# The input regions of a deformable convolution, turned once ahead of the loop instead of once in every step

## The reference

```python
x = x + _L0_conv_ref(_gn(x), ...)   # Fourier mixing along each axis plus a 1x1 mixing
x = x + _L1_conv_ref(_gn(x), ...)   # modulated deformable 3x3 convolution

# _L1_conv_ref, cut:
om   = conv3x3(x, w_om) + b_om              # 27 maps: dy, dx and a mask for each of 9 taps
mask = sigmoid(om[:, 18:])
ys, xs = dy + ky + row - 1, dx + kx + column - 1
vals = bilinear_sample(x, ys, xs) * mask    # 4 corners, zero outside the image
out  = einsum('bckhw,ock->bohw', vals, weight) + bias
```

## Time and profile before

| quantity | value |
|---|---|
| median of 3 runs | 2316.26 us (2314.34 to 2319.66) |
| profiled execution | 2315.21 us |
| its span, first to last instruction | 2313.2 us |
| mean granted TensorE clock | 0.968 |
| busy: PE, DVE, ACT, POOL | 1873.3, 1571.6, 1730.5, 1373.4 us |
| bytes moved by DMA | 363.82 MB, 58% of the engines' span |

### The profile page before, as it was taken

The page is one execution under the profiler, slowest core; times in us unless marked ns, Lnnn a source line. Parts: engine busy times, 40 slices in busy tenths (PEclk is TensorE's granted clock), DMA queues, the critical chain, the costliest instruction groups (busy, mean ns, idle before and its releaser), DMA issues. The chain is left out here.

```text
span 2313.2 us, 126528 instructions
## 1 busy us (share of the span) xinstructions
PE 1873.3 (81%) x50241; PEld 1302.3 (56%) x50241; DVE 1571.6 (68%) x2558; ACT 1730.5 (75%) x3238; POOL 1373.4 (59%) x1803
## 2 busy tenths in 40 slices
PE   8566178888888888888888888888888888888885
PEld 3411056666666666666666666666666666666663
DVE  8699166767676766676666666666666667676763
ACT  0003378888888888888888888888888888888884
POOL 0000066676667666766676676677667766766662
PEclk9599589999999999999999999999999999999997
DMA  8036536666666666666566666656665666666653
GB/s 323 1 127 281 224 90 158 157 154 157 159 152 158 156 161 152 156 156 162 151 157 154 153 159 156 160 153 156 156 161 152 157 158 155 157 156 159 153 155 89
DMA packets 196542, 363.82 MB, mean 157 GB/s; under 512 B 39760, under 2 KB 122480, under 8 KB 192368
## 3 DMA queue, kind: packets, MB, share of 16 engines
q1 hardware_dynamic: 196464, 362.74, 58.0%
HBM read 159.38 MB, written 52.22 MB: 91 GB/s over the span
## 5 line engine op out<-in xcount | busy, mean ns | idle before, releaser
L731 DVE COPY big<-pE 128x768 f32<-128x768 f32 x768 | 718.1, 935 | 190.3 <-PE pE L944 168.2
L478 POOL TENSOR_TENSOR halves<-prod,halves 128x300 f16<-128x300 f32 x768 | 604.0, 786 | 322.0 <-ACT halves L559 321.9
L565 ACT ACTIVATE big<-pE 128x768 f32<-128x768 f32 x768 | 632.2, 823 | 105.4 <-PE pE L944 100.0
L965 PE MATMUL pV<-big 128*32 128x144 f32 x16384 | 663.9, 291 | 7.2 <-issue 4.2
L469 POOL TENSOR_TENSOR prod<-big 128x300 f32<-128x300 f32 x768 | 550.2, 716 | 100.8 <-POOL big L493 32.2
L944 PE MATMUL pE<-big,sel_s 32*128 32x64 f16 (+1 forms) x24576 | 409.1, 202 | 241.4 <-DVE big L731 168.8
L944 PEld LDWEIGHTS pE<-big,sel_s 32*128 32x128 f16 x24576 | 325.7, 92 | 451.4 <-issue 311.8
L718 DVE STREAM_TRANSPOSE big<-halves 128x384 f32<-128x384 f32 x768 | 437.6, 570 | 173.3 <-POOL halves L478 171.3
L965 PEld LDWEIGHTS pV<-big 128*32 128x32 f32 x16384 | 436.4, 109 | 55.1 <-issue 10.1
L559 ACT ACTIVATE halves<-prod 128x300 f16<-128x300 f32 x768 | 452.9, 590 | 3.4 <-POOL prod L469 3.3
L493 POOL TENSOR_TENSOR big<-big,msk 128x360 f32<-128x360 f32 x128 | 105.0, 821 | 478.4 <-ACT big L579 478.4
(11 more groups left out here) (72 smaller groups left out, 1123.7 us busy)
## 6 DMA issues: line engine op xcount, KB each, us to landing
v<-big SPq DMA_DIRECT2D x1536, 96.0 KB
win<-xh_scratch SPq DMA_DIRECT2D x128, 544.0 KB, 4.2
big<-xh_scratch SPq DMA_DIRECT2D x384, 136.0 KB, 4.1
xh_scratch<-win SPq DMA_DIRECT2D x32, 544.0 KB, 2.7
big<-in_x SPq DMA_DIRECT2D x16, 1024.0 KB, 16.5
x_scratch<-big SPq DMA_DIRECT2D x16, 1024.0 KB, 3.9
x1r<-x_scratch SPq DMA_DIRECT2D x128, 128.0 KB, 2.1
out<-outs SPq DMA_DIRECT2D x128, 128.0 KB, 1.8
```

What stands on the lines that cost most here:

```text
L478: nc.gpsimd.tensor_tensor(half[:, rn % 2, :, 0:SQ, 1], prod[:, rn % 2, :, :], half[:, rn % 2, :, 0:SQ, 0], ALU.subtract).then_inc(low_done, 1)
L565: nc.scalar.activation(*expanded(1 - q, r, 0), ACT.Copy).then_inc(e_act, 1)
L731: nc.vector.tensor_copy(*expanded(1 - q, r, 1)).then_inc(e_dve, 1)
L965: last = mm(pV[r % 2][b * C:(b + 1) * C, o:o + TAPC], XT[q][:, t * P + b * C:t * P + (b + 1) * C], av[:, b * NT + t, :], start=True, stop= ...
```

## The change

The turned regions are made once, in the prologue, and stored in a new DRAM scratch `xw_d`: for each padded image row and each of the 8 columns of a strip one row of 17 strips x 128 channels. The strips with an even number stand first (nine of them), then the eight odd ones. The padding rows get zeroes from SP (four more transfers).

In the prologue, after ACT has normalised eight rows into `stg`, POOL copies them into strips, PE turns nine blocks (pairs of strips, the last one alone), and ACT copies these with three instructions into `xs`, from where SP stores them with two transfers of 64 partitions. PE now does these nine transposes, for two buffers, behind every fourth matmul of group 1's first block while group 0 is normalised; for group 1 they stand alone. SP starts the store of `xs` between one buffer's store into `xh_d` and the next one's.

In the loop the load of `win`, POOL's copy, PE's sixteen transposes and ACT's four copies of 128 x 512 are gone. In their place ACT starts four transfers, each 64 partitions of 1024 numbers, from `xw_d` straight into `XT`, at the head of a step, in front of its first copy. Line 965 waits for these instead of the copies, and takes its blocks in another order.

```diff
+            def cut_strips(g, j, q):
+                pool.wait_ge(xh_done, j * 2 + (g * N_XH + q + 1))
+                if not (isinstance(j, int) and j == 0 and g == 0):
+                    pool.wait_ge(xs_T, j * 2 + (g * N_XH + q - 1))
+                nc.gpsimd.tensor_copy(strips[:, q, :, :].rearrange("p s (r x) -> p r s x", r=XHR),
+                                      stg[:, q, :, :].rearrange("p r (s x) -> p r s x", x=TILE_C)) \
+                    .then_inc(strips_done, 1)
...
+            def turned(g, j, q):
+                act.wait_ge(xs_T, j * 2 + (g * N_XH + q + 1))
+                for k in range(EVEN // 4):
+                    nc.scalar.activation(xs[:, q, k * 512:(k + 1) * 512], pT[q][k][:, :], ACT.Copy)
+                nc.scalar.activation(xs[0:XHR * TILE_C, q, ODD * P:], pT[q][2][0:XHR * TILE_C, 0:P],
+                                     ACT.Copy).then_inc(xs_done, 1)
...
                 with act.Fori(first, N_XH // 2) as j:
                     for q in range(2):
                         act.wait_ge(xh_st[q], (j + g * (N_XH // 2)) * 16)
+                        act.wait_ge(strips_done, j * 2 + (g * N_XH + q - 1))
                         normalize(g, j, q)
+                    for q in range(2):
+                        act.wait_ge(xw_st[q], (j + g * (N_XH // 2)) * 32)
+                        turned(g, j, q)
...
+            def load_regions(n, q, place):
+                g, local = place(n)
+                wait(act, v_done, (n - 1) * len(VGROUPS))
+                act.nop(nofuse=True)
+                rows = xw_d[bass.ds((local * TILE_R + g * PADR) * TILE_C, REG_R * TILE_C), :]
+                left, right = XT[q][0:REG_R * TILE_C, :], XT[q][REG_R * TILE_C:P, :]
+                act.dma_start(left[:, 0:ODD * P], rows[:, ODD * P:2 * ODD * P]).then_inc(xt_ld[q], 16)
+                act.dma_start(left[:, ODD * P:], rows[:, 0:ODD * P]).then_inc(xt_ld[q], 16)
+                act.dma_start(right[:, 0:ODD * P], rows[:, 0:ODD * P]).then_inc(xt_ld[q], 16)
+                act.dma_start(right[:, ODD * P:], rows[:, EVEN * P:]).then_inc(xt_ld[q], 16)
+
             def step(N, q, on, place):
+                if on[1]:
+                    load_regions(N - 1, 1 - q, place)
...
-                    if on[1] and r in T_AT:
-                        k = T_AT.index(r)
-                        act.wait_ge(t_done, (N - 1) * 4 + (k + 1))
-                        nc.scalar.activation(XT[1 - q][:, k * 512:(k + 1) * 512], pR[:, :],
-                                             ACT.Copy).then_inc(xt_done, 1)
...
+            def transposes(g, j, q):
+                pe.wait_ge(strips_done, j * 2 + (g * N_XH + q + 1))
+                if not (isinstance(j, int) and j == 0 and g == 0):
+                    pe.wait_ge(xs_done, j * 2 + (g * N_XH + q - 1))
+                for t in range(EVEN):
...
+                    last = nc.tensor.transpose(pT[q][t // 4][0:rows, t % 4 * P:(t % 4 + 1) * P], pair, ident[:, :])
+                last.then_inc(xs_T, 1)
...
-                            pe.wait_ge(xt_done, n * 4 + 4)
+                            pe.wait_ge(xt_ld[q], (n - q) * 32 + 64)
```

More of the change, by code:

```diff
@@ L49 @@
 OM_AT, OMT_AT, CONV_AT = 0, 1, 4
-T_AT = (1, 2, 3, 5)
 HATS_AT = 2
@@ L60 @@
 XHR = 8
+STRIPS = PADC // TILE_C
+EVEN = (STRIPS + 1) // 2
+ODD = STRIPS // 2
 def v_count(act, gi):
@@ L221, in build @@
         pad_st = sem("pad_st")
-        win_ld = [sem(f"win_ld{i}") for i in range(2)]
+        strips_done = sem("strips_done")
+        xs_T = sem("xs_T")
+        xs_done = sem("xs_done")
+        xw_st = [sem(f"xw_st{i}") for i in range(2)]
+        xt_ld = [sem(f"xt_ld{i}") for i in range(2)]
         wino_ld = [sem(f"wino_ld{i}") for i in range(2)]
@@ L354, in _ @@
                                  zero[:, :]).then_inc(pad_st, 16)
+                    rows = xw_d[(g * PADR + edge) * TILE_C:(g * PADR + edge + TOP) * TILE_C, :]
+                    sp.dma_start(rows.rearrange("r n -> (r n)").rearrange("(p n) -> p n", p=P),
+                                 zero[:, :]).then_inc(pad_st, 16)
             for g in range(g_count):
@@ L543, in _ @@
                         normalize(g, 0, q)
+                    for q in range(2):
+                        turned(g, 0, q)
                     first = 1
@@ L915, in mix, with mixes @@
                    start=True, stop=True).then_inc(mix_done, 1)
-            for g in range(g_count):
-                first = 0
+            def transposes(g, j, q):
[3 more added lines that the diff above has]
+                for t in range(EVEN):
+                    pair = strips[:, q, 2 * t:min(2 * t + 2, STRIPS), :].rearrange("p s n -> p (s n)")
+                    rows = P if 2 * t + 1 < STRIPS else XHR * TILE_C
+                    last = nc.tensor.transpose(pT[q][t // 4][0:rows, t % 4 * P:(t % 4 + 1) * P], pair, ident[:, :])
+                last.then_inc(xs_T, 1)
+            MIXES = NXC // N_XH
+            for q in range(2):
+                mix(0, 0, q)
+            with pe.Fori(1, NXC // 2) as j:
+                for q in range(2):
+                    pe.wait_ge(x1_rows, j * 2 + (q - 1))
+                    mix(0, j, q)
+            for g in range(g_count):
+                def mixes(j, g=g):
+                    if g + 1 < g_count:
+                        for h in range(MIXES):
+                            for q in range(2):
+                                pe.wait_ge(x1_rows, j * (2 * MIXES) + ((g + 1) * NXC + 2 * h + q - 1))
+                                mix(g + 1, j * MIXES + h, q)
                 if g == 0:
+                    mixes(0)
                     for q in range(2):
-                        mix(g, 0, q)
-                    first = 1
-                with pe.Fori(first, NXC // 2) as j:
+                        transposes(g, 0, q)
+                with pe.Fori(int(g == 0), N_XH // 2) as j:
+                    mixes(j)
                     for q in range(2):
-                        pe.wait_ge(x1_rows, j * 2 + (g * NXC + q - 1))
-                        mix(g, j, q)
+                        transposes(g, j, q)
             pe.wait_ge(blocks_ld, 16 * NBLOCK)
@@ L1001, in step @@
                         last.then_inc(omT_done, 1)
-                    if on[1] and r in T_AT:
-                        n = N - 1
-                        t4 = T_AT.index(r)
-                        wait(pe, xt_done, n * 4 + t4)
-                        if t4 == 0:
-                            pe.wait_ge(strips_done, n + 1)
-                        for u in range(4):
-                            t = 4 * t4 + u
-                            last = nc.tensor.transpose(pR[:, u * P:(u + 1) * P],
-                                                       strips[:, t:t + 2, :, :].rearrange("p s r x -> p (s r x)"),
-                                                       ident[:, :])
-                        last.then_inc(t_done, 1)
             steps(pe, step)
```

44 lines of the change are left out of this document (23 added, 21 removed).

## The result

| quantity | before | after | shift32 (last experiment) |
|---|---|---|---|
| median of the runs, us | 2315.3 | 2412.3 | 2264.5 |
| lowest and highest | 2313.8 to 2319.7 | 2405.0 to 2414.8 (4 executions) | 2264.4 to 2264.6 (2 executions) |
| ratio to before, 95% interval | | 1.041 [1.038, 1.044] | 0.978 [0.977, 0.980] |
| span of the profiled run, us | 2313.2 | 2411.7 | 2262.5 |
| first copy to `om_s` starts at | 286.5 | 357.4 | 329.4 |

The change made the kernel 4.1% slower, where I had forecast 2.9% faster. Of the 98.5 us between the two spans 70.9 came before the first `om_s`, 26.1 in the 127 intervals after it and 1.4 at the end. (One sentence on the layout ahead of the prediction was wrong: in `xw_d` the eight odd strips stand first and then the nine even ones. No term hangs on it.)

What follows compares the result with a forecast made beforehand. No engine is full; a chain through PE, ACT, DVE, ACT, PE and DVE bounds the step. 2315.2 - 117 (loop) + 50 (prologue) = 2248 us, 2249 as the runs' median; range 2185 to 2365.

Steps and rivals of the forecast that it cites:

- The chain: Loop: path through PE, ACT, DVE, ACT, PE and DVE; removed work shortens the step by 0.93 us, 15.49 to 14.56.
- E1: Loop: second of TensorE's six expansions a step; stays 2.63 us after the first, if ScalarE's head is in time.
- E3: Loop: fourth of TensorE's six expansions a step; bound by DVE's grid subtraction, stays 7.72 us after the first.
- E4: Loop: fifth of TensorE's six expansions a step; bound by ScalarE, moves from 10.66 to 9.73 us after the first.
- the head: Start of ScalarE's step: four issues take 1.75 us, hidden with 0.1 to spare; at 0.63 each, E1 slips by 0.6.
- rival B: Loop: issuing from ScalarE is dearer; 2328 us at 0.63 us an issue, 2365 at 0.8; chance 0.15.
- The loads' bytes: Loop: 2.6 us of region loads into 2.45 us of free DMA time; 0.3 us of delay, hidden.
- Group 0's longer turns: Prologue: ScalarE's work of about 7.0 us a turn is hidden by 7.3 us of mixing; 2 us added.
- The burst: Prologue: the store of group 1's result, 8.4 MB at once, ahead of its first normalised rows; costs 21 us.
- Group 1's seven turns: Prologue: normalising turns grow from 4.27 to 8.5 us each, 30 us over seven.
- The last chain: End of the prologue: last chain and store, with the small padding transfers; -3 to +3 us.
- Rival A: Loop: region loads collide with the twelve copies, the final convolution waits, 0.3 us more a step; 2404 us; chance 0.15.

Runs made afterwards that it cites:

- shift32: The changed kernel with the edits of spread and pro, sixteen idle TensorE transposes a step in both groups, 32 more once ahead of group 1's loop; 2264.5 us.
- noloads: The changed kernel without the four region loads in the repeated steps, so old regions are multiplied; prologue unchanged; 2358.1 us.
- tiny: The changed kernel with the loop's four region loads still issued by ScalarE but cut to 16 numbers on 64 partitions; 2385.2 us.
- Nofill: noloads with sixteen idle transposes of the identity matrix a step on TensorE, at the places of the removed ones; 2441.0 us.
- g0: The changed kernel with the edits of spread and pro, and sixteen idle TensorE transposes a step only while group 0 is in the loop; 2298.9 us.
- spread: The changed kernel with ScalarE's four issues moved off the step's head: two behind its expansion copy of round 0, one each behind rounds 3 and 4; 2356.4 us.
- pro: The changed kernel with both buffers' `xh_d` stores ahead of those into `xw_d`, and group 1's 1 MB stores spread over group 0's loop; 2400.1 us.
- pad: The changed kernel with the edits of spread and pro, sixteen idle TensorE transposes a step in both groups, 128 more once ahead of group 1's loop; 2432.5 us.

## Why the prediction was wrong

- **What bounds the step, and what the removal gives: right.** The chain gives 0.9 us a step: 14.58 and 14.60 in shift32, 14.53 and 14.57 in noloads' steps at full clock, for 14.56 forecast. E1, E3, E4 and the final convolution lie where they were put, once the head is out of the way.
- **The head on ScalarE: the step that failed first and cost most, by its size.** I took 0.35 + 0.09 us for an issue and had 0.1 us to spare; with its gap it is 0.66 (2.64 / 4), near the dearer end of 0.63 that I had set down. E1 slipped by 0.52 and 0.94 in the steps shown, and tiny puts the cost at 0.6 us a step in group 0, just what the text gave for that end, and at 0.8 in group 1. The sign of being wrong that I had named, ScalarE's issues in front of an expansion, is what the trace shows. Of the two nearest rows I had chosen SyncE's single load; the twelve copies in a row were the like case, since four issues also stand in a row. That is rival B. It was the right one for this term, but its total, 2328, is still 84 us short, since it left the other terms as they were.
- **The rule on issuing.** The Trainium skill (DMA: Bandwidth & Descriptors, Issuing engines are not separate DMA queues) says that issuing from another engine saves only the sequencer's time, usually small against the transfer. By size the trace agrees, 0.5 us for an issue against a median of 5.6 to its landing. But here the small time was what counted: tiny, with next to no bytes, keeps 0.6 to 0.8 us of the cost a step.
- **A step I did not have: the clock.** I wrote that TensorE's 2.6 us of transposes buy nothing. But without them the granted clock fell in about a third of the steps of noloads (37 of 104), each 1.6 us longer, 0.5 to 0.6 us a step on the mean. Before, it fell in none of the 104. Nofill, g0 and shift32 show the cause by giving the work back. In the changed kernel it fell in 15 steps, each about 1 us longer, which makes 0.06 us a step in group 0 and 0.26 in group 1. So this term is small in the changed kernel, and grows when the other costs are taken away.
- **The loads' bytes.** Forecast 0.3 us of delay, hidden. TensorE's wait for the twelve copies grew from 16 to 49 us in all, and the bytes cost 27 us (after against tiny), though not wherever they stand: spread has them for nothing.
- **The loop, summed.** At full clock, group 0: 14.53 (noloads), + 0.61 for the issues (tiny), + 0.26 for the bytes (after), and + 0.06 for the clock, is 15.46. Group 1: 14.57 + 0.77 + 0.15 + 0.26 = 15.75. The gain of 0.9 is given back wholly, so the prologue stands uncovered.
- **The prologue: right in kind, 71 us in place of 50.** Group 0's longer turns put the start at + 10.6 (forecast 2; its turns are 8.9 us, not hidden by 7.3). The burst + 18.6 (forecast 21). Group 1's seven turns 7 x (9.35 - 4.27) = 35.6 (forecast 30). The last chain + 6 (forecast 0). Together 71, within the ends of 35 and 90. What I had not costed is ScalarE's wait for a store that stands behind the stores into `xw_d` in SyncE's list; pro takes 1.6 us a turn of it away.
- **Rival A** named nearly the time, 2404, but by luck: the copies' delay is there, at 27 us, while most of the loss came from the issues and the prologue, which it had left as forecast.
- **The range** ended at 2365. The head at 0.69 us a step, the mean of both groups, and the prologue as measured give 2249 + 87 + 21 = 2357. The other 55 us are about 26 for the bytes, which I had hidden (0.2 a step), 20 for the clock, for which I had no term (0.16 a step), and 7 at the change of groups (the twelve steps from the 61st take 196 us in the changed kernel, 190 before).

## What to carry to other kernels

Place DMA issues on a computing engine one or two at a time, where it would wait anyway: four in a row at the head of a step cost 0.6 to 0.8 us here, the same four spread over the step nothing. When work is taken from TensorE, look whether its granted clock still holds in the profile of after: the freed time may come back as slower matmuls, and an idle transpose can be worth its place. When a loop shows waits put down to "issue" of some us at a fixed rhythm, count the packets on the instruction queue before you look for a semaphore.

## What the runs showed of the hardware

- An issue from ScalarE takes 0.49 to 0.51 us (medians of L596 and L599), 0.66 with its gap. Four in a row hold ScalarE's computing back: it is idle for 2.38 us.
- Sixteen transposes fewer in a step of 15 us, with idle gaps of up to 1.44 us in the step shown, let TensorE's clock go to its lower level in about a third of the steps (noloads). Whether the gap starts it isn't settled, since the undisturbed step shown has one of 1.61 us at the same place.
- The same loop body stalls or not with its place in TensorE's code: shift32 has 96 idle transposes fewer in front of it than pad and is 168 us faster, of which the transposes themselves are 16 (0.66 / 4 each).
- Two transfers of 64 rows of 8 KB beside the copies went with longer waits for these than four of 64 rows of 4 KB (116 and 49 us in all).
